# A new hand-written order of the attention turn: where the row maxima, q and k products, statistics and stores stand in each engine's program

## The chip, the cores and the metric

One NeuronCore of one Trainium2 chip runs the whole program. The metric is the device time of one execution in microseconds (us). Five engines run their own instruction streams side by side: TensorE (PE, with its weight loads as PEld), VectorE (DVE), ScalarE (ACT), GpSimd (POOL), and SyncE (SP), which only issues DMAs. They meet through semaphores.

## The reference

A batch of 32 sequences of 512 tokens, 256 channels, float32:

```python
x = x + _layernorm(attn(_layernorm(x)))   # 16 heads of 16, 4 kv groups, rope, causal softmax
x = x + _layernorm(ffn(_layernorm(x)))    # x + shared expert + 2 of 16 experts by sigmoid gates
# attn:  q = rope(x Wq + bq), k = rope(x Wk + bk), v = x Wv + bv; k, v repeated over 4 heads
#        out = softmax(mask(q k^T / 4)) v Wo + bo
# ffn:   gates = sigmoid(x gate_w + gate_b); top 2, weights normalised to sum 1
```

## The kernel before

**Two phases.** `attention_phase` handles attention, the residual, the second layer norm, the router and the scatter of every token to its two experts' lists in DRAM. `expert_phases` then runs the expert tiles and the shared expert. The change touches the first phase alone.

**Turns.** The first phase is one software pipeline over the 32 sequences. Each engine's program is written out by the same loop: for each turn c from -3 to 33, go through the list `TURN`. One turn has 44 slots, (g, e), with g one of 4 kv groups and e one of 11 exponential units. In a full turn the softmax of sequence c stands beside the row maxima of c+1 (groups 1 to 3 of `M` in later slots; group 3 of the own sequence in g = 0), the q, k, v of c+2, the output projection and router of c-1, the scatter of c-2 and the first layer norm of c+3. Every engine is strictly in order, so a slot fixes what stands ahead of what on each engine. The steps of the list:

- `E` (g, e): PE makes scores transposed with the negated maximum already added (L728, L730), three PSUM buffers `ps_a`; ACT takes the exponential (L846).
- `M` (g, u), u = 0 to 5: PE makes the scores of 4 heads (or 2) (L712, L714) into one of two PSUM buffers `ps_d`; DVE reduces them to the row maximum (L966). `MAX_AT` gives each unit's slot.
- `P` (g, j): PE multiplies the exponentials with v (L742); ACT copies the heads out after the last (L889).
- `MISC` places the rest: `xt` (transposes of the normed input), `qe` 0 and 1 (the two halves of q, L758; DVE adds the bias and multiplies with the rope tables, L978), `kk` (k and v, L758; DVE L986, L989), `mt` 0 and 1 (maxima transposed, ACT L856, SP sends them into the operand `qs`), `ot`, `at`, `op` (attention output, L765, L793, L772; DVE L998, L1000, L1004), `ht`, `rg`, `rt` (router), `cn` (places in the lists, L777; DVE L1072 to L1095), `vt`.
- `SIDE` gives the slot of work without PE: DVE's statistics (L939, L947), `add_residual` (two sums of 128x512, L954), `choose`, `weigh_choice`; POOL's `split` (q and k cut into three bf16 parts: L589, L591 or L593, then L585, L587, L585, L587), `root` (L623 to L640), the scatters (L657) and `split_max` (L607 to L613); ACT's `norm` steps (L895); SP's loads and stores.

**Buffers that tie the engines.** `ps_d` has two buffers, so PE may start the n-th step for DVE only when DVE has finished the one two before it:

```python
                if number >= 2:
                    pe.wait_ge(d_taken, number - 1)
```

A scatter of 128 tokens is two indirect DMAs, issued by POOL; there are four scatters (`scatter0` to `scatter3`) in a turn. POOL's `split0a` waits until DVE has taken `qe` 1.

Of the kernel before, what the change touches and what calls it, by code (L numbers as in the profile page):

```python
# [62 lines left out]


MISC = {
    (0, 3): [("xt", 0, 2)],
    (0, 6): [("xt", 1, 2), ("ot", 0, -1), ("ot", 1, -1)],
    (0, 9): [("qe", 0, 2), ("cn", 0, -2), ("at", 0, -1), ("at", 1, -1)],
    (0, 10): [("op", 0, -1)],
    (1, 2): [("op", 1, -1)],  # L70
    (1, 4): [("qe", 1, 2)],
    (1, 7): [("mt", 1, 0)],
    (3, 0): [("kk", 0, 2), ("ht", 0, -1)],
    (3, 2): [("mt", 0, 1), ("ht", 1, -1)],
    (3, 4): [("rg", 0, -1)],
    (3, 7): [("rt", 0, -1)],
    (3, 10): [("vt", 0, 2)],
}

MAX_AT = [[1, 2, 2, 4, 8, 10], [0, 1, 4, 7, 8, 9], [2, 2, 5, 6, 9, 9], [0, 2, 3, 6, 7, 9]]  # L80
SUMS_AT = [10, 4]

SIDE = {
    "load_stacks": (0, 4),
    "load_x_res": (0, 6),
    "load_x": (0, 6),
    "store_q0": (2, 5),
    "store_h2": (3, 8),
    "store_q1": (3, 9),
    "store_k": (3, 10),  # L90
    "scatter0": (0, 9),
    "scatter1": (0, 9),
    "scatter2": (1, 1),
    "scatter3": (1, 3),
    "root_proj": (1, 1),
    "root_2": (2, 3),
    "root_1": (3, 9),
    "split0a": (1, 4),
    "split0b": (1, 7),
    "split0c": (2, 2),  # L100
    "split1a": (2, 4),
    "split1b": (2, 7),
    "split1c": (3, 5),
    "split2a": (3, 7),
# [12 lines left out]
    "plan_limits": (1, 4),
    "stats_proj_a": (1, 3),
    "stats_proj_b": (1, 3),
    "moments_proj": (1, 3),  # L120
    "add_residual_a": (1, 9),
# [4 lines left out]
    "stats_1_a": (2, 10),
    "stats_1_b": (2, 10),
    "moments_1": (3, 1),
    "choose": (3, 8),
# [36 lines left out]
def exists(b):  # L166
    return 0 <= b < B
# [13 lines left out]
A_NO = count_of(FOR_ACT)  # L181
# [132 lines left out]
def attention_phase(nc, a, v):  # L314
# [14 lines left out]
    with ctx:  # L329
# [6 lines left out]
        def sem(name):  # L336
            return ctx.enter_context(nc.semaphore(name))
# [67 lines left out]
        a_full, a_taken = sem("a_full"), sem("a_taken")  # L405
# [521 lines left out]
        def _(dve):  # L927
# [41 lines left out]
            def take(step, arg, b):  # L969
# [11 lines left out]
                elif step == "kk":  # L981
                    if b >= 1:
                        dve.wait_ge(split_steps, SPLITS * (3 * b - 1) + 1)
                    even, odd, both = slice(0, G * DH // 2), slice(G * DH // 2, G * DH), slice(0, G * DH)
                    for dst, src, k in ((roped_k[:, 0, :], both, 2), (roped_k[even, 1, :], odd, 3)):
                        dve.scalar_tensor_tensor(out=dst, in0=ps[src, :], scalar=bk[src, :], in1=rope[src, k, :],  # L986
                                                 op0=ALU.add, op1=ALU.mult)
                    dve.wait_ge(v_t_ready, b + 1)
                    dve.scalar_tensor_tensor(out=roped_k[odd, 1, :], in0=ps[even, :], scalar=bk[even, :],  # L989
                                             in1=rope[even, 3, :], op0=ALU.add, op1=ALU.mult).then_inc(d_taken, 1)  # L990
                elif step == "ot":
                    if arg == 0:
# [741 lines left out]
```

## Time and profile before

| | |
|---|---|
| median of 3 runs | 2605.22 us (2598.71 to 2606.5) |
| profiled execution | 2598.71 us, its span from first to last instruction 2596.9 us |
| share of the span busy | PE 92%, DVE 78%, POOL 63%, ACT 58% |
| granted TensorE clock, mean | 0.965 of full speed (2.4 GHz) |
| turns of the first phase | full turns from about 171 us to 1700 us, 53.4 or 54.9 us each, four of 56.5 to 58.5 us |
| second phase | from about 1850 us |

How to read it: PE's matmuls overlap one another in the records, so that a busy share near 1 does not say how fast it goes; the distance from one matmul's start to the next does. Idle time of an engine stands in square brackets in a timeline, with what ended it.

### The profile page before, as it was taken

How to read it: one execution, taken by the hardware profiler on the slowest of the kernel's cores; microseconds unless marked ns; L12 is line 12 of the kernel's file. 1: busy time of each engine (PE TensorE's matmuls, PEld its weight loads, DVE VectorE, ACT ScalarE, POOL GpSimd, SP SyncE). 2: the span in 40 equal slices, each digit the busy share in tenths (PEclk: the TensorE clock that was granted, in tenths of full speed). 3: DMA queues.
4: the chain of work that ended last, by engine and by line, in shares of the span. 5: the costliest groups of instructions: out<-in, count | busy, mean ns of one | idle time of the engine just before them, and what ended most of it. 6: DMA issues, size and time to landing. Idle time of an engine off the chain costs nothing. (4 is left out here: it accounts for less than half of the span.)

```text
span 2596.9 us, 60759 instructions
## 1 busy us (share of the span) xinstructions
PE 2386.5 (92%) x18798; PEld 1584.4 (61%) x18798; DVE 2025.7 (78%) x5220; ACT 1510.0 (58%) x3420; POOL 1646.0 (63%) x2761
## 2 busy tenths in 40 slices
PE   4999999999999999989999999996389999999997
PEld 2565566655666555555656665563268777877664
DVE  5688888888888888778888888873357777776887
ACT  1566666666766666665666766674134444444664
POOL 2457765666756666666676656734267666766887
PEclk7999999999999999999999999998689999999999
DMA  4354445444445444444443454331346546554997
GB/s 126 107 146 130 130 146 148 149 131 129 146 144 152 132 129 131 137 148 148 124 128 119 139 158 128 115 116 58 78 149 184 155 146 201 160 152 149 315 351 241
DMA packets 288652, 388.00 MB, mean 149 GB/s; under 512 B 27922, under 2 KB 238098, under 8 KB 288212
## 3 DMA queue, kind: packets, MB, share of 16 engines
q1 hardware_dynamic: 260788, 308.56, 40.3%
q0 software_dynamic: 27552, 75.57, 8.5%
q8 instruction: 161, 2.64, 0.4%
q14 instruction: 151, 1.24, 0.2%
HBM read 193.40 MB, written 172.27 MB: 141 GB/s over the span
## 5 line engine op out<-in xcount | busy, mean ns | idle before, releaser
L846 ACT ACTIVATE probs<-ps_a 128x512 f32<-128x512 f32 (+1 forms) x1408 | 718.8, 556 | 415.4 <-PE ps_a L730 398.3
L966 DVE TENSOR_REDUCE negmax<-ps_d 128x2 f32<-128x768 f32 (+3 forms) x768 | 776.9, 1038 | 130.7 <-PE ps_d L714 113.1
L712 PE MATMUL ps_d<-ks,qs 96*128 96x128 bf16 (+3 forms) x2048 | 487.8, 306 | 72.8 <-DVE negmax L966 49.0
L728 PE MATMUL ps_a<-qs,ks 99*128 99x512 bf16 (+3 forms) x2048 | 518.9, 306 | 8.2 <-ACT probs L846 4.4
L730 PE MATMUL ps_a<-mask_exp,ident_bf 128*128 128x128 bf16 x2048 | 398.7, 222 | 0.0
L714 PE MATMUL ps_d<-mask_max,ident_bf 128*128 128x128 bf16 x2048 | 395.5, 222 | 0.0
L1368 POOL DMA_INDIRECT y_dram<-ysb,to_row x286 | 282.4, 987 | 120.3 <-issue 86.3
L198 POOL TENSOR_TENSOR pool_cell<-zero_col 1x1 f32<-1x1 f32 x318 | 58.8, 185 | 463.5 <-DVE slot L1095 405.6
L712 PEld LDWEIGHTS ps_d<-ks,qs 96*128 96x128 bf16 x2048 | 203.4, 99 | 234.8 <-DVE negmax L966 76.2
L742 PE MATMUL ps_out<-probs,va 128*32 128x512 f32 (+3 forms) x4096 | 329.2, 439 | 0.0
L1441 PE MATMUL ps_gu<-wgu,rows_t 128*128 x1144 | 304.0, 389 | 7.1 <-DVE rows_t L1594 3.9
L728 PEld LDWEIGHTS ps_a<-qs,ks 99*128 99x128 bf16 x2048 | 203.1, 99 | 168.0 <-issue 53.9
L657 POOL DMA_INDIRECT sorted_dram<-h,slot x256 | 255.2, 997 | 69.4 <-issue 60.5
L1532 ACT ACTIVATE gate<-ps_gu 128x128 f32<-128x128 f32 x286 | 79.6, 278 | 271.1 <-issue 146.0
L1441 PEld LDWEIGHTS ps_gu<-wgu,rows_t 128*128 128x128 f32 x1144 | 200.6, 196 | 26.0 <-issue 9.4
L730 PEld LDWEIGHTS ps_a<-mask_exp,ident_bf 128*128 128x128 bf16 x2048 | 204.1, 100 | 20.1 <-issue 10.6
L714 PEld LDWEIGHTS ps_d<-mask_max,ident_bf 128*128 128x128 bf16 x2048 | 203.8, 99 | 1.1 <-issue 1.1
L1455 PE MATMUL ps_y<-wd,hid_t 128*128 x572 | 182.0, 400 | 20.9 <-ACT hid_t L1538 17.5
L742 PEld LDWEIGHTS ps_out<-probs,va 128*32 128x32 f32 x4096 | 107.1, 109 | 140.1 <-issue 97.0
L1601 DVE TENSOR_TENSOR hid<-ps_gu,gate 128x128 f32<-128x128 f32 x286 | 83.4, 291 | 123.0 <-ACT gate L1532 106.7
L1594 DVE COPY rows_t<-ps_t 128x256 f32<-128x256 f32 x286 | 118.9, 416 | 35.5 <-PE ps_t L1429 29.4
L585 POOL TENSOR_TENSOR q_parts<-rest,zero_col 128x512 bf16<-128x512 f32 x124 | 138.8, 1119 | 7.3
(200 smaller groups left out, 4585.9 us busy)
## 6 DMA issues: line engine op xcount, KB each, us to landing
qs<-q_stack_dram SPq DMA_DIRECT2D x128, 384.0 KB, 6.1
rows<-sorted_dram SPq DMA_DIRECT2D x286, 129.0 KB
y_in<-y_dram SPq DMA_DIRECT2D x32, 1024.0 KB
q_stack_dram<-q_parts SPq DMA_DIRECT2D x64, 384.0 KB
x_in<-in_x SPq DMA_DIRECT2D x32, 512.0 KB
q_stack_dram<-q_parts SPq DMA_DIRECT2D x64, 256.0 KB
x<-in_x SPq DMA_DIRECT2D x32, 512.0 KB
h_dram<-h SPq DMA_DIRECT2D x32, 512.0 KB, 3.0
```

The source lines that it names most:

```text
L585: steps.did(pool.tensor_tensor(parts[k], r, zero_col[0:n, :].to_broadcast([n, T]), ALU.add))
L657: pool.indirect_dma_start(out=sorted_dram[b // (B // 2)][:, :], in_=h2[:, k, j, :], in_offset=None, out_offset=bass.IndirectOffsetOnAxis(a ...
L712: pe.matmul(ps_d[:, number % 2, at:at + width], qs[0:KR, b % 2, h, j * P:(j + 1) * P], ks[0:KR, b % 2, g, 0:width], start=True, stop=False)
L714: ins = pe.matmul(ps_d[:, number % 2, at + j * P:at + (j + 1) * P], ident_bf[:, :], mask_max[:, :], start=False, stop=True)
L728: pe.matmul(ps_a[:, number % 3, at:at + width], ks[0:KM, b % 2, g, j * P:(j + 1) * P], qs[0:KM, b % 2, g * HG + h0 + k, j * P:T], start=Tr ...
L730: ins = pe.matmul(ps_a[:, number % 3, at:at + P], ident_bf[:, :], mask_exp[:, :], start=False, stop=True)
L742: ins = pe.matmul(ps_out[32 * h:32 * h + 32, j * P:T], va[:, b % 3, j, g * 32:(g + 1) * 32], probs[:, at:at + width], start=(j == 0), stop ...
L846: act.activation(probs[:, at:at + nh * width], ps_a[:, number % 3, 0:nh * width], ACT.Exp) \
L966: dve.tensor_reduce(negmax[:, g // 2, j, at:at + nh], src, AX_X, ALU.max, negate=True) \
L1368: pool.indirect_dma_start(out=y_dram[:, :], in_=ysb[:, k, :], in_offset=None, out_offset=bass.IndirectOffsetOnAxis(ap=to_row[k][:, 0:1].bi ...
L1441: ins = pe.matmul(ps_gu[:, t % 2, 0:2 * I], rows_t[:, t % 2, c, :], wgu[:, expert[t], c, :], start=(c == 0), stop=(c == NC - 1))
L1455: pe.matmul(ps_y[:, t % 2, 0:D], hid_t[:, t % 2, :], wd[:, expert[t], :], start=True, stop=True) \
```

## The change

It moves steps between slots; no operation is added or taken away, and no size changes. One wait of DVE ahead of `ot` is dropped.

```diff
 MISC = {
-    (0, 3): [("xt", 0, 2)],
-    (0, 6): [("xt", 1, 2), ("ot", 0, -1), ("ot", 1, -1)],
-    (0, 9): [("qe", 0, 2), ("cn", 0, -2), ("at", 0, -1), ("at", 1, -1)],
+    (0, 2): [("xt", 0, 2)],
+    (0, 5): [("xt", 1, 2)],
+    (0, 6): [("ot", 0, -1)],
+    (0, 7): [("ot", 1, -1)],
+    (0, 9): [("cn", 0, -2), ("at", 0, -1), ("at", 1, -1)],
     (0, 10): [("op", 0, -1)],
-    (1, 2): [("op", 1, -1)],
-    (1, 4): [("qe", 1, 2)],
-    (1, 7): [("mt", 1, 0)],
-    (3, 0): [("kk", 0, 2), ("ht", 0, -1)],
-    (3, 2): [("mt", 0, 1), ("ht", 1, -1)],
+    (1, 1): [("op", 1, -1)],
+    (1, 7): [("qe", 0, 2), ("qe", 1, 2), ("mt", 1, 0)],
+    (2, 9): [("kk", 0, 2)],
+    (3, 2): [("ht", 0, -1), ("ht", 1, -1)],
     (3, 4): [("rg", 0, -1)],
-    (3, 7): [("rt", 0, -1)],
-    (3, 10): [("vt", 0, 2)],
+    (3, 7): [("mt", 0, 1), ("vt", 0, 2)],
+    (3, 8): [("rt", 0, -1)],
 }
-MAX_AT = [[1, 2, 2, 4, 8, 10], [0, 1, 4, 7, 8, 9], [2, 2, 5, 6, 9, 9], [0, 2, 3, 6, 7, 9]]
+MAX_AT = [[0, 0, 1, 3, 8, 10], [0, 1, 3, 6, 8, 9], [0, 1, 4, 6, 7, 9], [1, 1, 3, 7, 8, 8]]
 SIDE = {
-    "load_stacks": (0, 4),        "load_x": (0, 6),
+    "load_stacks": (0, 5),        "load_x": (0, 5),
-    "store_q0": (2, 5),   "store_h2": (3, 8),   "store_q1": (3, 9),   "scatter1": (0, 9),
+    "store_q0": (2, 4),   "store_h2": (3, 10),  "store_q1": (3, 10),  "scatter1": (0, 10),
-    "root_proj": (1, 1),  "root_2": (2, 3),     "root_1": (3, 9),
+    "root_proj": (1, 2),  "root_2": (2, 6),     "root_1": (3, 10),
-    "split0a": (1, 4),    "split0b": (1, 7),
+    "split0a": (1, 2),    "split0b": (1, 9),
-    "split1a": (2, 4),    "split1b": (2, 7),    "split1c": (3, 5),    "split2a": (3, 7),
+    "split1a": (2, 7),    "split1b": (3, 2),    "split1c": (3, 7),    "split2a": (3, 9),
-    "norm_proj_a": (1, 7),     "norm_proj_b": (1, 7),
+    "norm_proj_a": (1, 9),     "norm_proj_b": (1, 9),
-    "weigh_choice_a": (0, 0),  "weigh_choice_b": (0, 1),   "plan_limits": (1, 4),
+    "weigh_choice_a": (0, 2),  "weigh_choice_b": (0, 5),   "plan_limits": (1, 3),
-    "stats_proj_a": (1, 3),    "stats_proj_b": (1, 3),     "moments_proj": (1, 3),
+    "stats_proj_a": (1, 2),    "stats_proj_b": (1, 4),     "moments_proj": (1, 5),
-    "add_residual_a": (1, 9),  "stats_2_b": (1, 10),
+    "add_residual_a": (1, 10), "stats_2_b": (2, 0),
-    "stats_1_a": (2, 10),      "stats_1_b": (2, 10),       "moments_1": (3, 1),  "choose": (3, 8),
+    "stats_1_a": (3, 4),       "stats_1_b": (3, 4),        "moments_1": (3, 6),  "choose": (3, 10),
 }
@@ DVE, step "ot" @@
                         post.begin(b)
-                        if exists(b + 3):
-                            dve.wait_ge(a_taken, A_NO["xt", 1, b + 3] + 1)
```

Unchanged entries are left out and several stand on one line. `scatter0` (0, 9), `scatter2` (1, 1), `scatter3` (1, 3), `split0c` (2, 2), `add_residual_b` and `stats_2_a` (1, 10), `moments_2` (2, 4), `norm_2` (2, 10), `norm_1_a` (3, 8), `norm_1_b` and `split2b`, `split2c` (3, 10) stay.

## Rows read from the trace of the kernel before

**Rows 1.** The page: span and busy time by engine.

```profile
span 2596.9 us, 60759 instructions
PE 2386.5 (92%) x18798; PEld 1584.4 (61%) x18798; DVE 2025.7 (78%) x5220; ACT 1510.0 (58%) x3420; POOL 1646.0 (63%) x2761
```

**Rows 2.** Windows, one whole turn each: us, busy by engine, PEclk, DMA.

```profile
1324.30:1377.70 53.40, 51.71 (x485) 32.48 (x483) 46.13 (x101) 36.14 (x73) 35.45 (x59) 1.00 0.46 135
1377.70:1432.60 54.90, 53.24 (x485) 33.39 (x483) 46.07 (x101) 36.19 (x73) 36.48 (x60) 0.97 0.44 132
```

**Rows 3.** PE's timeline in the turn from 1324.30.

```profile
1349.69 0.38 PE L712 MATMUL ps_d<-ks,qs 96*128 96x512 bf16 x1
...
1353.53 0.38 PE L728 MATMUL ps_a<-qs,ks 99*128 99x512 bf16 x1
1353.92 0.39 PE L728 MATMUL ps_a<-qs,ks 99*128 99x512 bf16 x1
1354.40 0.39 PE L728 MATMUL ps_a<-qs,ks 99*128 99x512 bf16 x1
...
1357.21 0.34 PE L728 MATMUL ps_a<-qs,ks 99*128 99x384 bf16 x1
...
1358.84 0.34 PE L712 MATMUL ps_d<-ks,qs 96*128 96x384 bf16 x1 [1.24 <-DVE negmax L966]
...
1359.97 0.34 PE L712 MATMUL ps_d<-ks,qs 96*128 96x384 bf16 x1 [0.29 <-DVE negmax L966]
...
1365.50 1.93 PE L758 MATMUL ps_d<-h1t,wkv 128*128 128x512 f32 x4
1367.27 0.60 PE L797 MATMUL ps_a<-ident,h 128*128 128x128 f32 x4
```

**Rows 4.** DVE's timeline in the same turn.

```profile
1330.97 0.36 DVE L998 RECIPROCAL denom<-ps_d 128x32 f32<-128x32 f32 x1 [0.81 <-PE ps_d L765]
1331.37 0.69 DVE L1000 TENSOR_TENSOR h_heads<-ps_d,denom 128x512 f32<-128x512 f32 x1
...
1348.25 1.28 DVE L978 SCALAR_TENSOR_TENSOR roped_q<-ps_d,bq,rope 128x1024 f32<-128x1024 f32 x1
1349.45 3.35 DVE L966 TENSOR_REDUCE negmax<-ps_d 128x2 f32<-128x768 f32 x3
1352.94 3.82 DVE L954 TENSOR_TENSOR x<-proj,x 128x512 f32<-128x512 f32 x2
1356.79 1.41 DVE L939 BATCH_NORM_STATS2 stats<-x 128x6 f32<-128x256 f32 x4
1358.12 1.80 DVE L966 TENSOR_REDUCE negmax<-ps_d 128x4 f32<-128x512 f32 x2
```

**Rows 5.** POOL's timeline in the same turn.

```profile
1351.08 1.09 POOL L657 DMA_INDIRECT sorted_dram<-h,slot  x1 [0.29 <-POOL shift L640]
1352.48 0.97 POOL L657 DMA_INDIRECT sorted_dram<-h,slot  x1 [0.30 <-issue]
1353.47 1.28 POOL L589 TENSOR_TENSOR rest<-roped_q 128x512 f32<-128x512 f32 x1
1354.83 1.38 POOL L585 TENSOR_TENSOR q_parts<-rest,zero_col 128x512 bf16<-128x512 f32 x1
...
1357.86 1.04 POOL L585 TENSOR_TENSOR q_parts<-rest,zero_col 128x512 bf16<-128x512 f32 x1
```

**Rows 6.** The line of the residual (L954): all, and after 1720 us.

```profile
L954 DVE TENSOR_TENSOR x<-proj,x x64: 682/1524/2374, 147.4 to 1811.9; 128x512 f32<-128x512 f32 x64
...
L954 DVE TENSOR_TENSOR x<-proj,x x6: 682/688/693, 1725.5 to 1811.9; 128x512 f32<-128x512 f32 x6
```

**Rows 7.** DVE's and POOL's timelines near 1725 us, where no split follows the scatter.

```profile
1725.49 1.29 DVE L954 TENSOR_TENSOR x<-proj,x 128x512 f32<-128x512 f32 x2 [0.29 <-ACT proj L895]
...
1725.03 0.97 POOL L657 DMA_INDIRECT sorted_dram<-h,slot  x1 [0.30 <-issue]
```

**Rows 8.** ACT's timeline: the norm of the projection.

```profile
1350.83 2.08 ACT L895 ACTIVATE proj<-proj,shift,rstd 128x256 f32<-128x256 f32 x4 [0.69 <-POOL shift L640]
```

More of the change, by code:

```diff
@@ L65 @@
 MISC = {
-    (0, 3): [("xt", 0, 2)],
-    (0, 6): [("xt", 1, 2), ("ot", 0, -1), ("ot", 1, -1)],
-    (0, 9): [("qe", 0, 2), ("cn", 0, -2), ("at", 0, -1), ("at", 1, -1)],
-    (0, 10): [("op", 0, -1)],
-    (1, 2): [("op", 1, -1)],
-    (1, 4): [("qe", 1, 2)],
-    (1, 7): [("mt", 1, 0)],
-    (3, 0): [("kk", 0, 2), ("ht", 0, -1)],
-    (3, 2): [("mt", 0, 1), ("ht", 1, -1)],
+    (0, 2): [("xt", 0, 2)],
[3 more added lines that the diff above has]
+    (0, 9): [("cn", 0, -2), ("at", 0, -1), ("at", 1, -1)],
+    (0, 10): [("op", 0, -1)],
+    (1, 1): [("op", 1, -1)],
+    (1, 7): [("qe", 0, 2), ("qe", 1, 2), ("mt", 1, 0)],
+    (2, 9): [("kk", 0, 2)],
+    (3, 2): [("ht", 0, -1), ("ht", 1, -1)],
     (3, 4): [("rg", 0, -1)],
-    (3, 7): [("rt", 0, -1)],
-    (3, 10): [("vt", 0, 2)],
+    (3, 7): [("mt", 0, 1), ("vt", 0, 2)],
+    (3, 8): [("rt", 0, -1)],
 }
-MAX_AT = [[1, 2, 2, 4, 8, 10], [0, 1, 4, 7, 8, 9], [2, 2, 5, 6, 9, 9], [0, 2, 3, 6, 7, 9]]
+MAX_AT = [[0, 0, 1, 3, 8, 10], [0, 1, 3, 6, 8, 9], [0, 1, 4, 6, 7, 9], [1, 1, 3, 7, 8, 8]]
 SUMS_AT = [10, 4]
 SIDE = {
-    "load_stacks": (0, 4),
+    "load_stacks": (0, 5),
     "load_x_res": (0, 6),
[L86 to L89, printed above, removed]
+    "load_x": (0, 5),
+    "store_q0": (2, 4),
+    "store_h2": (3, 10),
+    "store_q1": (3, 10),
     "store_k": (3, 10),
     "scatter0": (0, 9),
-    "scatter1": (0, 9),
+    "scatter1": (0, 10),
     "scatter2": (1, 1),
     "scatter3": (1, 3),
[L95 to L99, printed above, removed]
+    "root_proj": (1, 2),
+    "root_2": (2, 6),
+    "root_1": (3, 10),
+    "split0a": (1, 2),
+    "split0b": (1, 9),
     "split0c": (2, 2),
[L101 to L104, printed above, removed]
+    "split1a": (2, 7),
+    "split1b": (3, 2),
+    "split1c": (3, 7),
+    "split2a": (3, 9),
     "split2b": (3, 10),
     "split2c": (3, 10),
-    "norm_proj_a": (1, 7),
-    "norm_proj_b": (1, 7),
+    "norm_proj_a": (1, 9),
+    "norm_proj_b": (1, 9),
     "norm_2_a": (2, 10),
@@ L112 @@
     "norm_1_b": (3, 10),
-    "weigh_choice_a": (0, 0),
-    "weigh_choice_b": (0, 1),
+    "weigh_choice_a": (0, 2),
+    "weigh_choice_b": (0, 5),
     "plan_ends": (0, 9),
     "plan_tiles": (1, 0),
[L117 to L121, printed above, removed]
+    "plan_limits": (1, 3),
+    "stats_proj_a": (1, 2),
+    "stats_proj_b": (1, 4),
+    "moments_proj": (1, 5),
+    "add_residual_a": (1, 10),
     "add_residual_b": (1, 10),
     "stats_2_a": (1, 10),
-    "stats_2_b": (1, 10),
+    "stats_2_b": (2, 0),
     "moments_2": (2, 4),
[L126 to L129, printed above, removed]
+    "stats_1_a": (3, 4),
+    "stats_1_b": (3, 4),
+    "moments_1": (3, 6),
+    "choose": (3, 10),
 }
```

## The prediction

> **What bounds the kernel now.** The page first [rows 1]: PE is busy for 2386.5 us of the 2596.9 and DVE for 2025.7. A busy share says little of PE, so I cut the first phase into its turns with the windows view [rows 2]. Most full turns take either 53.4 or 54.9 us; the longer ones show a granted clock of 0.97 instead of 1.00, which is a stretch at 1.2 GHz for 1.5 us more. DVE is busy for 46.1 us of either. There are 28 full turns (c = 2 to 29) of sequences alike.
>
> Then PE's timeline in one 53.4 us turn [rows 3]. I give times as offsets from the turn's start, 1324.30. PE runs without a hole up to the maxima of slot (1, 8), at 25.4. Behind them it falters: three exponential units start 0.39, 0.48 and 0.29 apart, where 0.28 is the unhindered distance, and then it waits for DVE's maxima, so that steps 0.22 apart start 1.63 and 0.67 apart. That is 0.1 + 0.2 + 1.4 + 0.45, with 0.2 ahead of the first unit and 0.1 later: 2.4 us lost in this stretch and some 0.3 us in the rest of the turn. PE alone would need 50.7 us.
>
> Why DVE is late stands in its timeline [rows 4]: at offset 28.6 it begins the residual, two sums, which take 3.82 us; then statistics, and the maxima for which PE waits only come behind them. The line's own view shows that this is not what the sums need [rows 6]: a median of 1524 and up to 2374 ns over all, 682 to 693 after 1720 us. POOL's timeline has the reason [rows 5]: while DVE sums, POOL works on tensors in SBUF. The first sum starts at 28.64 and can't end before POOL's subtraction (29.17 to 30.45) is over; the second waits for POOL's next. Near 1725 us no split follows the scatter, and two sums take 1.29 us together although an indirect DMA runs beside them [rows 7]. So the two engines exclude one another on such instructions, and indirect DMAs don't count. The turn is PE's 50.7 us plus what this collision makes PE wait.
>
> **The change part by part.** The number of instructions and their sizes don't change, so PE's 50.7 us stay. The question is only how far PE slips behind its own pace.
>
> *Start of the turn.* Maxima go one slot earlier and `weigh_choice` later. PE's `ot` 0 ends at 6.6 at its new offset, DVE is through with its four maxima and the weights by then (they fill 6.0 us of the timeline now), and takes 0.36 + 0.69 us for it [rows 4], so it is done by 7.8; PE wants its buffer for the next maxima at 7.9. At most 0.1 us is lost here. `qe` 0 leaves this part, and `op` follows the counts directly; between them PE's positions only move by the 1.77 us of one q product (the k product has that distance [rows 3]). The dropped wait costs and gains nothing: PE's `ot` stands behind `xt` 1 anyway.
>
> *The two q products side by side.* The steps ahead of slot (1, 8) are the same set as before, so PE reaches it at the same offset, 25.3. Back from there, `qe` 1 starts at 22.85, lasts 1.97, and DVE takes it from 24.9 to 26.15 (1.28 [rows 4]). Two maxima follow (three take 3.35 us [rows 4], the narrow one 0.95 of it) and end at 28.5. The earlier of the two buffers is free in time for each; nothing is lost.
>
> *ACT's norm of the projection* moves behind one more pair of exponentials, to slot (1, 9). Its last exponential ends near 26.9, and the norm takes 2.08 us [rows 8], so that DVE's residual can start at 29.0, 0.4 later than now. In exchange PE's 0.3 us of faltering at the exponentials goes, since these are now taken in time.
>
> *POOL.* It is in order, and `split0a` now stands ahead of `scatter3`, waiting for `qe` 1 until 26.15. So: 1.28 us of split to 27.5, 0.29 of idle, the first indirect DMA 1.09, 0.30 of idle, the second from about 29.2 to 30.2 [rows 5], and at once `split0b` (1.04). The scatters ahead of it and `root_proj` end near 24.5, in time.
>
> *The residual, then, against POOL.* This decides. The first sum (29.0) starts 0.2 us before the second indirect DMA. Before the change it started 0.46 us after that DMA's start and still lost to the tensor instruction that stood behind the DMA, though that one only starts 0.53 us later in the records [rows 4, 5]. POOL must have had its claim in as soon as the DMA was under way. By that, the first sum now wins and ends at 29.6, the second finds the claim of `split0b` and waits until 31.2, and with its last 0.56 us ends at 31.8. The Trainium skill ("SBUF — State Buffer", "SBUF: two separate sides") calls the shared port pair an exclusive lock that whichever instruction starts first holds for the whole of it. The exclusion agrees with rows 4 to 6; "starts first" does not agree with the recorded starts there, 0.53 us the other way.
>
> *From there to the k product.* DVE: two statistics (0.7) to 32.5, M(1,0) done 33.2, two statistics 33.8, M(1,1) done 35.0, M(1,2) 35.8, moments (0.3), M(1,3) 37.0, M(1,4) 38.2 [rows 4]. PE may start M(1,2) when M(1,0) is done: it wants to at 32.2 and slips 1.0; M(1,3) behind M(1,1): slip 1.95; M(1,4) behind M(1,2): 2.15. New is that `kk` stands at (2, 9), inside the stretch where DVE is behind, and waits for M(1,4): slip 2.7. After it PE works 1.77 us on a product and DVE catches up; statistics of x, now at (3, 4), fall into DVE's idle time there. What stood in their old place saves DVE 1.35 us, but only after `kk`.
>
> *The rest.* `mt` 0 goes from (3, 2) to (3, 7); it is copied, sent and needed 4.8 us later at the next turn's start, where `mt` 1 now has 4.5 and costs PE 0.2 at most. POOL's `root_1` goes behind `split2a` and ends 0 to 0.3 us before ACT wants it for `norm_1_a`. If POOL were 1 us later there, ACT would stand still for that time, with three `ps_a` buffers of cover. The stores and loads of the stacks shift by under 1 us, with over 2 us of room before group 0's maxima. In sum the turn loses 2.7 us instead of 2.4 + 0.3: 53.4 us, as before. Holes of 2.7 us as close together as now let the clock fall about as often.
>
> **The rivals.** (A) The forecast above, no change: 2598.7 us of the profiled execution, give or take 15 us, which is 0.5 us a turn for steps that I placed by 0.2 or 0.3 us each. (B) Both sums win. The second starts at 29.6, before the recorded start of `split0b` at 30.2. If POOL's claim is not made before 0.4 us into its last DMA, or by any rule that goes by recorded starts, the residual ends at 30.2, PE slips only 1.1 us in the turn (M(1,3) 0.3, M(1,4) 0.5, `kk` 1.1). That is 1.6 us less in 28 turns, 45 us, and the lower clock of some third of the turns would largely go, another 10: 2545 us. By the skill's rule, named above, it would be this case. For it: the claim is only bounded, somewhere in the first 0.5 us. Against: the one geometry that the trace has went POOL's way in all full turns. (C) Both sums lose: if the norm ends 0.3 us later, or POOL's scatter 0.3 us earlier than I placed them, the first sum meets a claimed port, waits for `split0b` to 31.2, ends at 31.8, and the second waits for a further subtraction and ends at 33.4. PE slips 4.3 us by `kk`: 1.6 us more in 28 turns, 45 us, 2645 us. It decides from a shift of 0.2 to 0.3 us between ACT and POOL, which is the uncertainty of both chains. This is the case on the slow side. (D) The edits don't act at all: excluded where DVE is the limit.
>
> **How the numbers follow.** A 0.45, B 0.22, C 0.28, others (ACT standing before `root_1`, a stack late, the four long turns with the pad rows coming out otherwise, 15 us among them) 0.05. A measurement tells 0.3%, 8 us, from no change. A is centred on no change with a spread of 15 us: 0.17 faster, 0.15 same, 0.13 slower. With B and C: faster 0.41, same 0.17, slower 0.42. The runs' median is 2605.2 us, 6.5 above the profiled execution, and a new median should lie between: 2602 us. The range holds A and most of B and C: 2540 to 2655; A alone would be 2587 to 2618.
>
> **What would show it.** In the trace after: the residual line's durations. About 690 ns for the first sum and 2200 for the second is A; 690 for both is B; both over 2000 is C. PE's waits for DVE at L712 between offsets 32 and 38, four smaller ones instead of two, and one at L758 ahead of the k product. POOL's `split0a` directly behind DVE's second q step. The turn's length by windows: 53.4, 51.8 or 55.0. I am wrong in kind if PE waits elsewhere: for ACT at the end of a turn, or for `ot`'s buffer near offset 8.

## The result, and the profile of the kernel after

The change makes the kernel slower by 0.9%: 2626.75 us (median of 4 runs, 2620.0 to 2629.71) against 2605.86 of the kernel before beside it, ratio 1.0091 with a 95% interval of 1.0068 to 1.0113. Run once more in another job (e13 below) it gave 1.0060 (1.0040 to 1.0080). The forecast was no change, 2602 us.

The page and the windows of two full turns stand first. The page: span and busy time.

```profile
span 2619.1 us, 60730 instructions
PE 2389.8 (91%) x18798; PEld 1576.4 (60%) x18798; DVE 1981.9 (76%) x5220; ACT 1510.6 (58%) x3420; POOL 1637.4 (63%) x2761
```

Windows of the kernel after, columns as in [rows 2]: two full turns, and the turns 17 to 21 together.

```profile
1341.70:1395.80 54.10, 52.12 (x488) 32.40 (x485) 44.48 (x103) 36.21 (x74) 35.20 (x59) 1.00 0.45 134
1395.80:1449.80 54.00, 51.98 (x487) 32.31 (x483) 44.34 (x101) 36.09 (x74) 35.08 (x59) 1.00 0.45 133
...
sum 294.50, PE 268.10 PEld 167.66 DVE 226.43 ACT 181.18 POOL 191.59; mean PE 53.62 PEld 33.53 DVE 45.29 ACT 36.24 POOL 38.32
```

The same five turns of the kernel before, as one sum of windows:

```profile
sum 285.80, PE 264.65 PEld 165.71 DVE 233.84 ACT 181.17 POOL 191.84; mean PE 52.93 PEld 33.14 DVE 46.77 ACT 36.23 POOL 38.37
```

DVE is busy for 44 us less in all and PE ends 22.2 us later. A full turn at full clock takes 54.04 us (from its first E matmul to the next turn's) instead of 53.41 [rows 2]. But in turns 2 to 16 the kernel before had 8 stretches at the lower clock (54.9 us turns), the kernel after 4. So those fifteen turns take 813.7 us before and 815.1 after. The 22.2 us lie here: turns -2 to 1 +6.7, turns 2 to 16 +1.4, turns 17 to 21 +8.7, turns 22 to 29 +3.6, the rest +1.8. These are net figures. At full clock a full turn is 0.63 us longer, which is 14.5 us over the 23 plain ones (turns 2 to 16 and 22 to 29); the lower clock, met less often, gave back 9.5 of them. Of the 8.7 us of turns 17 to 21, 3.2 are the same 0.63 us again and 4.3 fell in turn 18 alone (58.6 us before, 62.9 after). So the longer full turn is the largest part, 17.6 us over all 28, and the start the next.

One full turn after, from 1341.70. First PE: the maxima M(0,3) and the heads' product P(0,3), both q products, and the waits further on.

```profile
1361.04 0.86 PE L743 MATMUL ps_out<-probs,va 128*32 128x256 f32 x16
...
1362.67 0.22 PE L715 MATMUL ps_d<-mask_max,ident_bf 128*128 128x128 bf16 x1
...
1365.17 1.98 PE L759 MATMUL ps_d<-h1t,wq 128*128 128x512 f32 x4 [0.28 <-DVE negmax L967]
...
1367.76 0.38 PE L713 MATMUL ps_d<-ks,qs 96*128 96x512 bf16 x1
...
1375.48 0.34 PE L713 MATMUL ps_d<-ks,qs 96*128 96x384 bf16 x1 [0.64 <-DVE negmax L967]
1377.27 0.34 PE L713 MATMUL ps_d<-ks,qs 96*128 96x384 bf16 x1 [0.72 <-DVE negmax L967]
1380.40 1.98 PE L759 MATMUL ps_d<-h1t,wkv 128*128 128x512 f32 x4 [0.31 <-DVE negmax L967]
```

DVE's timeline in the same turn:

```profile
1364.16 0.96 DVE L967 TENSOR_REDUCE negmax<-ps_d 128x2 f32<-128x768 f32 x1 [0.82 <-PE ps_d L715]
...
1367.19 1.28 DVE L979 SCALAR_TENSOR_TENSOR roped_q<-ps_d,bq,rope 128x1024 f32<-128x1024 f32 x1 [0.89 <-PE ps_d L759]
...
1371.44 2.61 DVE L955 TENSOR_TENSOR x<-proj,x 128x512 f32<-128x512 f32 x2 [0.57 <-ACT proj L896]
```

POOL's, with `scatter1` and `scatter2` now four indirect DMAs in a row:

```profile
1358.23 0.99 POOL L658 DMA_INDIRECT sorted_dram<-h,slot  x1 [0.15 <-issue]
1359.53 0.96 POOL L658 DMA_INDIRECT sorted_dram<-h,slot  x1 [0.31 <-issue]
1360.79 0.96 POOL L658 DMA_INDIRECT sorted_dram<-h,slot  x1 [0.30 <-issue]
1362.06 0.96 POOL L658 DMA_INDIRECT sorted_dram<-h,slot  x1 [0.30 <-issue]
...
1371.45 0.97 POOL L658 DMA_INDIRECT sorted_dram<-h,slot  x1 [0.30 <-issue]
1372.43 1.06 POOL L586 TENSOR_TENSOR q_parts<-rest,zero_col 128x512 bf16<-128x512 f32 x1
```

and ACT's copy of the heads behind P(0,3):

```profile
1364.01 0.59 ACT L890 COPY heads_t<-ps_out 128x512 f32<-128x512 f32 x1 [2.35 <-remote]
```

The collision came as forecast in case A: of the two sums in the 2.61 us, the first took 728 ns and the second 1955, and PE waits at M(1,2), M(1,3) and the k product. What was not forecast stands ahead of it. M(0,3) ends at 1362.89 by the records and DVE, idle since 1363.33, takes it at 1364.16, 1.27 us after that end. P(0,3) ends at 1361.90 and ACT, idle, copies at 1364.01, 2.11 us after. For most steps of the turn an idle engine starts 0.04 to 0.07 us behind PE's end. Both late starts come after POOL's row of four indirect DMAs has ended (1363.02). Through them the second q product waits 0.28 us, M(0,4) starts at offset 26.06 instead of 25.39 [rows 3], and the residual at 29.74 instead of the forecast 29.0.

A row of four is not new: the kernel before has one too (`scatter0` and `scatter1`), further ahead in its turn. POOL's last DMA of it, PE's second `op`, and DVE's start behind that:

```profile
1343.07 0.96 POOL L657 DMA_INDIRECT sorted_dram<-h,slot  x1 [0.30 <-issue]
```

```profile
1342.41 1.94 PE L772 MATMUL ps_d<-wo,headst_h2t 128*128 128x256 f32 x8
```

```profile
1344.85 0.69 DVE L1004 TENSOR_TENSOR proj<-ps_d,bo 128x512 f32<-128x512 f32 x1 [1.02 <-PE ps_d L772]
```

DVE starts 0.50 us after PE's recorded end there, and ACT's copy behind P(0,3) comes 0.4 us late in most full turns. So late starts were there before the change; the change moved the row to where they are longer and where M(0,3) and P(0,3) stand.

The start, in windows (turns -1 and 0), of before and then of after:

```profile
24.50:72.60 48.10, 25.72 (x126) 13.03 (x126) 32.50 (x48) 2.78 (x6) 16.07 (x24) 0.71 0.42 127
72.60:119.00 46.40, 44.25 (x401) 25.82 (x400) 31.56 (x39) 29.59 (x59) 23.71 (x34) 0.97 0.38 107
```

```profile
23.40:73.70 50.30, 25.98 (x127) 13.21 (x126) 33.06 (x48) 2.98 (x6) 15.52 (x21) 0.66 0.38 112
73.70:124.10 50.40, 47.40 (x401) 27.42 (x402) 31.89 (x39) 28.76 (x57) 22.71 (x35) 0.90 0.36 104
```

In turn -1 PE has little to do and stands for the first stacks, 15.3 us before. The first q product stood ahead of that wait and now stands behind it, and turn 0 runs at a granted clock of 0.90 instead of 0.97.

### The profile page after: what moved, and what is told of

Same layout as the page of the kernel before. It is cut to its first block and busy times, and to the rows that moved or that the text cites. A ratio compares the mean times of both kernels' runs of the same rounds, so it can differ in the third digit from the quotient of the medians.

```text
span 2619.1 us, 60730 instructions
## 1 busy us (share of the span) xinstructions
PE 2389.8 (91%) x18798; PEld 1576.4 (60%) x18798; DVE 1981.9 (76%) x5220; ACT 1510.6 (58%) x3420; POOL 1637.4 (63%) x2761
## 5 line engine op out<-in xcount | busy, mean ns | idle before, releaser
L847 ACT ACTIVATE probs<-ps_a 128x512 f32<-128x512 f32 (+1 forms) x1408 | 736.8, 561 | 354.1 <-PE ps_a L731 288.0
L729 PE MATMUL ps_a<-qs,ks 99*128 99x512 bf16 (+3 forms) x2048 | 525.4, 304 | 1.4 <-ACT probs L847 0.3
L1440 PEld LDWEIGHTS ps_gu<-wgu,rows_t 128*128 128x128 f32 x1144 | 200.1, 195 | 30.6 <-issue 14.5
L1621 DVE SCALAR_TENSOR_TENSOR ysb<-ps_y,rows,half_row 128x256 f32<-128x256 f32 x286 | 138.4, 484 | 9.7 <-PE ps_y L1454 3.6
```

Source lines behind the costliest of these rows:

```text
L729: pe.matmul(ps_a[:, number % 3, at:at + width], ks[0:KM, b % 2, g, j * P:(j + 1) * P], qs[0:KM, b % 2, g * HG + h0 + k, j * P:T], start=Tr ...
L847: act.activation(probs[:, at:at + nh * width], ps_a[:, number % 3, 0:nh * width], ACT.Exp) \
L1440: ins = pe.matmul(ps_gu[:, t % 2, 0:2 * I], rows_t[:, t % 2, c, :], wgu[:, expert[t], c, :], start=(c == 0), stop=(c == NC - 1))
L1621: dve.scalar_tensor_tensor(out=ysb[:, k, :], in0=ps_y[:, t % 2, 0:D], scalar=rows[:, t % RD, D + 1:D + 2], in1=half_row[:, t % 2, :], op0= ...
```

## The experiments

Ratios are to the kernel before, run beside each kernel in its job. "The wait" is one line in `split`, ahead of POOL's next step against the residual; `x1_ready` counts finished sums.

**e1: POOL waits for the residual, in the kernel after.**

```diff
+                if stage == 1 and unit == 0 and 0 <= b - 3 < B:
+                    pool.wait_ge(x1_ready, 2 * (b - 2))
```

> The kernel after, and POOL waits for both sums of the residual before it begins the split of the k heads' first part (split0b). Port theory (the turn after loses its time because the second sum stands behind a subtraction of POOL, 728 and 1955 ns in the turn from 1341.7): both sums take about 690 ns, the residual 1.4 us in all, the maxima behind it come 1.3 us sooner, PE's waits for DVE in slots (1, 8) to (2, 9) mostly go (0.64 + 0.72 + 0.31 + what the steps between them lose), so a full turn goes from 54.0 to 52.4 us, and over 28 turns some 45 us come off: about 2580 us. Rival (late signals: the turn after lost its 0.6 us because PE's signals reach DVE 1 to 2 us late behind four indirect DMAs in a row, and the residual only fills time that PE lacks anyway): the sums shorten, but DVE's later start of the maxima stays; 53.5 us or more a turn, under 15 us off in all.

2585.76 us, 0.9918 (0.9899 to 0.9936). Both sums take 732 and 679 ns, and a full turn 52.67 us instead of 54.04. The port theory holds: the blocked sum costs 1.37 us a turn. Some of the gain is lost in turn 18, which takes 71.5 us here and 62.9 in the kernel after; it holds a DMA wait that differs from run to run (see e14 and the section on the forecast).

**e2: the same in the kernel before**, with `stage == 0`, ahead of `split0a`.

> The kernel before, and POOL waits for both sums of the residual before it begins split0a, which stands next to the residual there. Port theory: the two sums of 3.82 us become 1.4, PE's 1.24 and 0.29 us of waiting for the maxima go with what the steps between lose (2.4 us in the turn), and a turn is 53.4 - 2.0 = 51.4 us, 28 turns 55 us less: about 2545 us. If the collision costs PE nothing net (POOL's chain, later by up to 1.3 us, becomes what is waited for: root_2, split0c or split1), the turn stays at 53 us or more, 2590 us or more.

2584.96 us, 0.9907 (0.9889 to 0.9926). The sums take 693 and 684 ns, and M(1,5) comes 1.77 us sooner, but a full turn takes 53.31 us: only 0.1 less than a turn at full clock before. What the whole gains is that no turn up to 16 is of the 54.9 us kind now. ACT's timeline, PE's and POOL's show where the 1.77 us went:

```profile
1359.69 1.58 ACT L897 ACTIVATE h<-x,shift,rstd 128x256 f32<-128x256 f32 x3 [1.98 <-POOL shift L642]
```

```profile
1361.90 0.63 PE L799 MATMUL ps_a<-ident,h 128*128 128x128 f32 x4 [0.57 <-ACT h L897]
1364.61 0.38 PE L817 MATMUL ps_a<-ident_bf,negmax_parts 128*24 128x128 bf16 x4 [0.85 <-POOL negmax_parts L615]
```

```profile
1350.28 1.27 POOL L591 TENSOR_TENSOR rest<-roped_q 128x512 f32<-128x512 f32 x1 [0.96 <-DVE x L956]
```

POOL begins its row of splits and roots at offset 30.3 instead of 29.15, and works without a hole of note to the root that the norm of x needs. ACT waits for POOL, and PE for both.

**e8: e2, and `ht` 0 and `mt` 0 to later slots.**

```diff
-    (3, 0): [("kk", 0, 2), ("ht", 0, -1)],
-    (3, 2): [("mt", 0, 1), ("ht", 1, -1)],
+    (3, 0): [("kk", 0, 2)],
+    (3, 2): [("ht", 0, -1), ("ht", 1, -1)],
-    (3, 7): [("rt", 0, -1)],
+    (3, 7): [("mt", 0, 1), ("rt", 0, -1)],
```

> The kernel before with POOL's wait (e2), and ht 0 moved from (3, 0) to (3, 2) and mt 0 from (3, 2) to (3, 7), as in the change. In e2 the shorter residual brought PE 1.77 us by slot (2, 9), and PE gave 0.57 us of it back waiting for ACT at ht 0 and 0.85 us waiting for POOL's split of the maxima at mt 0. If those two places are where the gain went, the full turns go from 53.3 to about 51.9, 28 turns 39 us less: about 2545 us. If POOL's later chain binds at other places too (split1, the norm of the next sequence), 52.5 or more.

2585.65 us, 0.9935 (0.9905 to 0.9965), full turns of 53.34. The expectation fell. PE's 0.85 us at `mt` 0 are gone, but at `ht` it now waits 0.52 us for ACT's exponentials and early in the turn 0.48 us for DVE, and ACT waits 0.96 us instead of 0.37 for POOL at the norm of the next sequence. The two places only showed the limit; that POOL's chain of about 53.3 us sets it is what e15 tests.

**e15: the kernel before, third scatter behind the root** (`"scatter2": (1, 2)`).

> The kernel before with the third scatter behind the root of the projection. POOL's root ends near 26.0, two scatters follow to 31.3, and split0a begins at 31.4 instead of 29.2; both sums (28.6 and 29.2) come before POOL's last indirect DMA and take 690 ns each. Theory drawn from e2 and e8 (there POOL worked without a hole from the residual to the norm of x and set a turn of 53.3): its row of work now begins 1.1 us later than in e2, so the turn is 53.3 to 54.4 and the kernel no faster than before, 2590 to 2630 us. Rival (the port alone is what cost the kernel before its 2.4 us a turn, as the forecast had it): turns of 51.7, about 2555 us.

2632.85 us, 1.0078 (1.0060 to 1.0096). Full turns take 54.4 or 55.0, with both sums undisturbed (DVE) and ACT waiting 3.11 us for POOL, whose split begins at 31.4 or 32.0:

```profile
1377.22 1.28 DVE L954 TENSOR_TENSOR x<-proj,x 128x512 f32<-128x512 f32 x2
```

```profile
1390.05 2.08 ACT L895 ACTIVATE h<-x,shift,rstd 128x256 f32<-128x256 f32 x4 [3.11 <-POOL shift L640]
```

The turn's length follows POOL one for one: the split begins 1.13 or 1.73 us later than in e2, and the turns are 1.13 or 1.72 us longer. The whole came out just above the expected 2590 to 2630 us. With e2 and e8 this shows that in the old order POOL's chain is a second bound right under the collision. Freeing DVE alone gives nearly nothing.

**e3: the first q product back in (0, 9), in the kernel after.**

```diff
-    (0, 9): [("cn", 0, -2), ("at", 0, -1), ("at", 1, -1)],
+    (0, 9): [("qe", 0, 2), ("cn", 0, -2), ("at", 0, -1), ("at", 1, -1)],
-    (1, 7): [("qe", 0, 2), ("qe", 1, 2), ("mt", 1, 0)],
+    (1, 7): [("qe", 1, 2), ("mt", 1, 0)],
```

> The kernel after with one part undone: the first q product stands in slot (0, 9) again. If the start-up pays for its move (turn -1 took 50.25 us after and 48.09 before, PE stood for 17.92 us at one place instead of 15.29), 2 us come back at the start. If M(0, 3)'s late signal (1.27 us in the full turns) delays the second of two q products side by side, the full turns gain the 0.3 to 0.5 us by which DVE's second q step came late: 54.0 to 53.6 us, 10 us in all. Together about -12 us, 2615 us. If the pair of q products was not at fault, only the 2 us of the start.

2603.35 us, 0.9992 (0.9975 to 1.0009): this one move is worth the whole 0.9%. It also gave a comparison that no one had to build: full turns of two lengths side by side, at full clock. Windows:

```profile
1372.40:1424.80 52.40, 52.06 (x488) 32.33 (x484) 43.05 (x102) 36.13 (x74) 35.03 (x59) 1.00 0.47 138
1424.80:1478.80 54.00, 51.99 (x488) 32.42 (x485) 44.22 (x103) 36.01 (x74) 35.05 (x59) 1.00 0.45 134
```

DVE's residual in each, then POOL beside it:

```profile
1401.79 1.29 DVE L955 TENSOR_TENSOR x<-proj,x 128x512 f32<-128x512 f32 x2 [0.44 <-issue]
...
1454.66 2.41 DVE L955 TENSOR_TENSOR x<-proj,x 128x512 f32<-128x512 f32 x2 [0.57 <-ACT proj L896]
```

```profile
1402.05 1.27 POOL L658 DMA_INDIRECT sorted_dram<-h,slot  x1 [0.30 <-issue]
1403.33 1.06 POOL L586 TENSOR_TENSOR q_parts<-rest,zero_col 128x512 bf16<-128x512 f32 x1
...
1454.48 0.96 POOL L658 DMA_INDIRECT sorted_dram<-h,slot  x1 [0.30 <-issue]
1455.47 1.05 POOL L586 TENSOR_TENSOR q_parts<-rest,zero_col 128x512 bf16<-128x512 f32 x1
```

In the short turn the second sum starts 0.34 us after POOL's last indirect DMA and takes 684 ns; in the long one it starts 0.8 us after and takes 1806. The turns differ by 1.6 us, the forecast's distance from case A to B. With the residual's 0.5 us goes the heads' copy behind P(0,3), which comes 1.0 to 1.8 us after PE's end in the short turns and 2.4 or 2.5 in the long ones. What decides between the two is not shown.

**e5: e1 and e3 together.**

> The kernel after with both of the edits that gained alone: POOL waits for the residual before split0b (e1), and the first q product stands in (0, 9) again (e3). e3 had full turns of two kinds, 52.4 us where both sums took 690 ns and 54.0 where the second took 1810. If the port alone makes the difference between them, all full turns are now 52.4 or, as e1's 0.2 us wait at the second q product goes too, 52.2; over e1 (52.66) that is 8 to 13 us and 2 us at the start: about 2573 us. If the two edits gain the same time twice (the q products' DVE step late only moved the residual), it stays at e1's 2586.

2570.91 us, 0.9871 (0.9827 to 0.9914). The total is what was expected, but not for the reasons given: full turns take 52.85, longer than e1's, since `mt` 1 waits 0.51 us for ACT behind the late heads' copy. The gain over e1 is the start (157.6 us for turns -2 to 1 instead of 164.1) and turn 18 (61.4 instead of 71.5).

**e4: the k product back in (3, 0), in the kernel after.**

> The kernel after with one part undone: the k product stands in slot (3, 0) again, behind the maxima of group 2. If its place inside the stretch where DVE is behind costs PE what its wait shows (0.31 us in the turn from 1341.7, and by the forecast 0.55 us more slip than at M(1, 4)), the full turns gain 0.3 to 0.5 us, 8 to 14 us in all, about 2615 us. If the slip is only handed on to the next maxima, no change within 0.2%.

2657.64 us, 1.0208 (1.0181 to 1.0235), the other way: full turns of 55.2. The maxima of group 2 had been pulled forward with the k product. With the product right ahead of them, PE waits for DVE to take k before it may start M(2,1):

```profile
1410.61 0.28 PE L713 MATMUL ps_d<-ks,qs 96*128 96x256 bf16 x1 [1.61 <-DVE roped_k_v_t L990]
```

**e6 and e9: the third scatter behind POOL's root of the projection**, e6 with e1's wait and e9 without.

```diff
-    "scatter2": (1, 1),
-    "root_proj": (1, 2),
+    "scatter2": (1, 2),
+    "root_proj": (1, 1),
```

> As e1, and the third scatter goes behind POOL's root of the projection, so that no more than two indirect DMAs stand in a row beside PE's signals of P(0, 3) and M(0, 3), where e1 has four. Theory of late signals (a row of indirect DMAs keeps PE's signals from the engines that wait): the heads' copy behind P(0, 3) and the maxima behind M(0, 3), which start 2.03 and 1.18 us after the matmul's end in e1, start under 0.5 us behind it; the maxima come 0.7 us sooner, PE's 0.2 us wait at the second q product goes, and the turn is 52.3 to 52.5 instead of 52.66. Rival (the delay belongs to the place in the turn, not to the row): both stay above 1 us. A cost that may hide the gain: split0a and the last scatter come 0.4 us later.

> The kernel after with one move: the third scatter stands behind POOL's root of the projection, as in e6, but without the wait of POOL for the residual. It tells whether the row of four indirect DMAs is the first cause, and the lost second sum its consequence. In e6 the sums began at 29.2 and 29.8 and POOL's last indirect DMA at 30.2, so that both were ahead of it, and POOL's wait cost nothing. If that holds without the wait, full turns take 52.2 us instead of 54.0, and the whole is about 2565 us. If the wait was what saved the sums, one of them takes over 1500 ns again and a turn is 53.5 or more, about 2605 us.

e6: 2566.35 us, 0.9836 (0.9791 to 0.9881). e9: 2567.32 us, 0.9841 (0.9821 to 0.9860). Both have full turns of 52.17 us, all alike. In e9's turn from 1306.0, PE, then DVE, ACT and POOL:

```profile
1325.28 0.86 PE L743 MATMUL ps_out<-probs,va 128*32 128x256 f32 x16
...
1326.91 0.22 PE L715 MATMUL ps_d<-mask_max,ident_bf 128*128 128x128 bf16 x1
```

```profile
1335.13 1.29 DVE L955 TENSOR_TENSOR x<-proj,x 128x512 f32<-128x512 f32 x2 [0.57 <-ACT proj L896]
```

```profile
1326.20 0.59 ACT L890 COPY heads_t<-ps_out 128x512 f32<-128x512 f32 x1 [0.30 <-PE ps_out L743]
```

```profile
1323.76 0.96 POOL L658 DMA_INDIRECT sorted_dram<-h,slot  x1 [0.30 <-issue]
1327.66 0.20 POOL L624 TENSOR_TENSOR var<-moments,eps 128x4 f32<-128x4 f32 x1 [2.94 <-DVE moments L948]
...
1336.12 1.14 POOL L658 DMA_INDIRECT sorted_dram<-h,slot  x1 [0.30 <-issue]
1337.28 1.05 POOL L586 TENSOR_TENSOR q_parts<-rest,zero_col 128x512 bf16<-128x512 f32 x1
```

The copy now follows P(0,3)'s end (1326.14) by 0.06 us instead of 2.11, and DVE's start behind M(0,3) is not late either. The residual begins at offset 29.2, a microsecond ahead of POOL's last indirect DMA, both sums run free, and the wait is not needed. What the late starts cost by themselves is the distance from e1 to e6, where both sums are free in either: 0.50 us a turn. The other 1.37 us of the 1.87 is the blocked sum. Breaking up the row frees it too, but e9 moves two things toward that: the first sum comes 0.5 us sooner (the late starts gone), and POOL's last indirect DMA 0.4 us later (30.14 instead of 29.75, since the third scatter now stands behind the root). That the blocked sum was a consequence of the late starts alone is therefore not shown.

**e10: e9 with e3's move and the pads of e7 (below).**

> As e9, with the pad rows apart (e7) and the first q product in (0, 9) again (e3, e5). The pads took 11 us off the turns 19 to 21 in e7 and the place of the q product 5 to 7 us off the start in e3 and e5; in e5 the full turns lost 0.5 us by ACT's heads copy coming 2.4 us behind P(0, 3), a late signal that e9's move should take away. If the three are independent: e9 less 16 to 18 us, about 2548, and full turns of 52.2 or less. If the q product in (0, 9) makes the full turns longer by itself, they are over 52.4 and the whole is above 2553.

2607.28 us, 1.0001 (0.9989 to 1.0012), full turns of 53.81, the slow rival. With the q product ahead of `cn`, the places in the lists come later, and POOL's work behind them too, the first scatter by 2.7 us and the last by 2.3. Its `split0a` now meets the first sum, as in the kernel before (DVE, then POOL):

```profile
1363.56 2.37 DVE L956 TENSOR_TENSOR x<-proj,x 128x512 f32<-128x512 f32 x2 [0.57 <-ACT proj L897]
```

```profile
1363.50 1.28 POOL L591 TENSOR_TENSOR rest<-roped_q 128x512 f32<-128x512 f32 x1
```

**e7: the pad rows apart, in the kernel after.** Turns 18 to 21 each hold four more indirect DMAs, which fill the lists' ends.

```diff
+PAD_AT = ((0, 2), (1, 2), (2, 5), (3, 10))
-                    if B // 2 + 2 <= c < B // 2 + 6 and at in ((0, 2), (0, 4), (0, 6), (0, 8)):
-                        pad(4 * (c - B // 2 - 2) + at[1] // 2 - 1)
+                    if B // 2 + 2 <= c < B // 2 + 6 and at in PAD_AT:
+                        pad(4 * (c - B // 2 - 2) + PAD_AT.index(at))
```

> The kernel after, and the four indirect DMAs of pad rows in each of the turns 18 to 21 no longer stand in a row at the start of the turn but singly: in (0, 2), behind the root of the projection in (1, 2), in (2, 5) and in (3, 10), where POOL has idle time. These turns and turn 17 took 294.5 us after and 285.8 before, against 270 for five plain ones. If rows of indirect DMAs are what delays PE's signals (7.3 and 6.1 us in turn 18, 2.9 in turns 19 to 21), the five turns take 275 to 280 and the whole 15 to 20 us less, about 2610 us. If the long turns come from something else (the experts' weights, the store that the first pad waits for), they stay above 290.

2606.12 us, 0.9998 (0.9979 to 1.0017). Turns 19 to 21 take 54.4 to 54.7 us instead of 58.1 to 58.5, turn 18 stays at 62.7. There PE waits for something else:

```profile
1066.92 0.27 PE L714 MATMUL ps_d<-ks,qs 96*128 96x128 bf16 x1 [6.15 <-DMA qs<-q_stack_dram]
```

**e11: e10, and the pad row's two stores one turn earlier** (`if c == E:` for `if c == E + 1:`).

> As e10, and SP issues the two stores of the pad row one turn earlier. Turn 18 took 58.6 us before, 62.9 after and 62.7 with the pads apart (e7), and its first pad began at 10.7 us behind the store. If the wait for the store makes turn 18 long (the pads can't run in POOL's idle time at the turn's start, so that they stand in a row with the scatters), it takes 53 to 55 us as its neighbours do in e7, and the whole 7 to 9 us less than e10. If turn 18 is long for the experts' weights or the plan, nothing changes.

2606.00 us, 0.9992 (0.9981 to 1.0004). Turn 18 takes 64.6 us, e10's 66.3: it was not that store.

**e14: e9, the pads apart, and the first plan's store by SP moved from the start of turn 18, ahead of the stacks' loads, to slot (1, 4).**

> e9 (the third scatter behind the root) with the pads apart (e7), and SP stores the first half's plan in slot (1, 4) of turn 18 instead of at its start, ahead of the stacks' loads. Full turns 52.2 as in e9. Turns 19 to 21 took 57.1, 58.1 and 58.1 in e9; apart, 53 each, as e7's were 0.5 over its plain turns: 14 us less. If the plan's store is what held up the stacks in turn 18 (6.2 us of PE's waiting in e7), that turn goes from 62.3 to 54 to 56. Together 2543 to 2547 us. If turn 18 stays at 60 or more, it was not the plan's store, and the sum is 2552.

2561.14 us, 0.9803 (0.9784 to 0.9823). Windows of turns 18 and 19:

```profile
1017.60:1072.30 54.70, 52.11 (x488) 32.35 (x485) 43.41 (x102) 35.20 (x72) 37.82 (x60) 1.00 0.55 144
1072.30:1128.60 56.30, 52.56 (x488) 32.35 (x485) 44.39 (x102) 35.88 (x73) 39.08 (x63) 1.00 0.46 138
```

Turn 18 falls from 62.3 (e9) to 54.7. In e7, with the pads apart alone, it had not moved, and in e17 and e18 below, which also move the store, it takes 56.4 and 57.1, where every run without that edit has 58.6 or more. So the plan's store was its cause. Turns 19 to 21 stay at 56.3, where 53 were expected: in this order POOL has no hole late in the turn, and PE waits 0.8 to 0.9 us for ACT at three places behind the pads.

**e17, e18: e14 with two pads at the start of each of eight turns**, slots (0, 2) and (0, 4) of turns 18 to 25; the same kernel in two jobs.

> e14 with the sixteen pad rows otherwise: two in each of the turns 18 to 25, both at the turn's start in slots (0, 2) and (0, 4), where POOL has over 9 us of idle time in e9, instead of four singly in four turns. In e14 the turns 19 to 21 still took 56.3 against 52.2, with PE waiting 0.8 to 0.9 us for ACT at three places, as the pad in (3, 10) stands ahead of the root that ACT's norm waits for, and those in (1, 2) and (2, 5) push POOL's splits. If that is their cost, two pads in idle time cost under 0.5 us a turn: turns 18 to 25 take 53.5 for turn 18 and 52.2 to 52.7 for the others, and the whole is 2545 to 2550. If a row of two already delays PE's signals by 2 us, as four do, they take 54 or more and it is 2557 or above.

> e17's kernel once more. In e17's job the kernel before took 2560 us instead of 2606 and the second phase 738 us instead of 764 to 772, so that the length of its turns can't be held against e14's. If the kernel before comes out near 2606 here and the turns 19 to 25 still take 52.2 to 52.7, two pads in idle time cost nothing, and the whole is 2545 to 2550, a ratio of 0.976 to 0.979. If the turns 19 to 25 take 53.5 or more here, it was the job that made them short, and a row of two already has a price.

2511.56 us, 0.9803 (0.9782 to 0.9825), and 2515.75 us, 0.9812 (0.9799 to 0.9825). The kernel before took 2560 and 2563 us in these two jobs, so the ratios alone can be held against the others. Turns 19 to 25 take 52.17 to 52.24 in both, like the plain ones, and turns -2 to 32 end 12 to 15 us sooner than e14's; what follows them took 738 and 741 us, and 763 to 772 in all other jobs. Two pads in idle time cost nothing in these two jobs. That can't be held against e14, for in these two jobs, which ran on other chips than the rest, no start is late. Of 1236 and 1241 waits of ACT and DVE for PE the latest ends 0.15 and 0.13 us after PE's recorded end, in the second phase too. In each of the other traces 83 to 163 such waits end later than 0.15 us, the latest 1.35 to 2.75. ACT in the same place of turn 12, behind the same row of two, first in e14 (0.62 us after PE's end at 731.62) and then in e17 (0.03 us after 730.39):

```profile
732.24 0.60 ACT L852 ACTIVATE probs<-ps_a 128x512 f32<-128x512 f32 x1 [0.73 <-PE ps_a L736]
```

```profile
730.42 1.08 ACT L851 ACTIVATE probs<-ps_a 128x512 f32<-128x512 f32 x2 [0.36 <-PE ps_a L735]
```

The 46 us that the kernel before took less there, and the shorter second phase, would fit, but neither of the two kernels compared was profiled in such a job, and the kernel after was not run in one. So whether the change costs 0.9% where no start is late is open, and so is why the ratio is no better than e14's.

**e12, e16, e13: the dropped wait of DVE back, twice, and the kernel after once more.**

> The kernel after with the dropped wait of DVE ahead of ot put back, all else as after. By the forecast it costs and gains nothing, since PE's ot stands behind xt 1 in either order: ratio to after 1.000, 2625 us give or take 5. If DVE's wait for ACT delays ot's start (the maxima of group 3 stand behind it), a turn gets 0.1 us longer or more, 2629 or above.

> The kernel after, unchanged, beside the others of this job. If the first measurement holds: ratio to before 1.007 to 1.011. If the job matters more than its interval says, it comes out near e12's 1.004.

> The kernel after with DVE's dropped wait put back, once more, beside e13. If the wait costs and gains nothing, its ratio to before is within 0.2% of e13's; if it saves 0.5% as e12 suggested, it is 0.4 to 0.6% below e13.

With the wait: 2617.59 us, 1.0038 (1.0025 to 1.0052), and 2623.67 us, 1.0048 (1.0032 to 1.0063). Without it, beside the latter: 2628.17 us, 1.0060 (1.0040 to 1.0080). The intervals overlap, full turns are 53.96, 54.04 and 54.04 us: no difference can be told. The first measurement of the kernel after (1.0068 to 1.0113) lies above both of those with the wait, but its own repeat came out 0.3% lower, so the job matters as much.

## Why the forecast was wrong, step by step

**"Two q products side by side, nothing is lost": the step that failed.** It holds the full turn at 53.4 us; measured are 54.04, and 0.63 us in 28 turns are 17.6 of the 22.2 us. PE reached M(0,4) 0.67 us late, because DVE and ACT started 1.3 and 2.1 us late behind POOL's row of four indirect DMAs. The forecast had no term for that, though the kernel before shows starts 0.3 to 0.5 us late around its own row. With the row broken up (e9) the same two products side by side cost nothing, and with them apart but the row kept (e3) 14 of the 23 plain full turns still take 53.9 to 54.1 us.

**The sum's reach: failed too.** 28 full turns were costed, and the rest was left unchanged, with the long turns only a part of a spread. The start cost 6.7 us. It is not chance: turns -2 to 1 took 164 to 168 us in eleven runs with both q products at (1, 7) (172 in e4), 159 to 162 in the four with the old order, and 158 to 164 in those with `qe` 0 back (e3, e5, e10, e11). It was in reach of the profile before: a windows row for turn -1, and the question what stands ahead of the long wait there. Of the 8.7 us in turns 17 to 21 less can be laid to the change. Turn 18, 4.3 of them, took 62.9 to 66.3 us in four runs of the new order without other edits that touch it (after, e12, e13, e16), and in the four of the old order 58.6, 64.6, 67.2 and 70.8 (before, e8, e15, e2), so its 4.3 us lie within the spread of one DMA wait.

**"The clock falls about as often": failed, and hid part of the rest.** 8 turns in turns 2 to 16 before, 4 after, and one more before in the turns behind 21. This gave back 9.5 us. That the whole came out only 0.9% from "no change" is in that part luck.

**The residual against POOL: right.** "The first sum wins, the second waits": 690 and 2200 ns forecast, 728 and 1955 measured, alike in the other full turns, and PE's waits at the three steps named. Case B, both free, was forecast at 1.6 us a turn less and came so in e3 (1.6), at 52.17 in e9 against a forecast of 51.8. Case C, both lost, came nowhere; in e10 the first sum alone is lost. The forecast took the claim to be made at once or within 0.4 us of POOL's DMA; e3's free sum at 0.34 us and the lost one of before at 0.46 [rows 4, 5] put it between. That A came is in part luck: by the forecast's own times the second sum starts 0.4 us behind POOL's DMA, where neither run decides, and by the trace 0.65 us behind, since the first sum slipped by 0.7 us and the DMA by 0.55.

The Trainium skill ("SBUF — State Buffer", "SBUF: two separate sides") has the pair go to the operation that starts first. In e3's short turn and in e9 that agrees with the records. It does not for the sum that loses in e3's long turn, which starts 0.2 us ahead of the split in the records.

**"The turn is PE's 50.7 us plus what this collision makes PE wait": wrong for the kernel before.** e2 took the collision away there and the turn fell by 0.1 us. A timeline shows which wait ends last, not which chain comes next; POOL's row was not summed. The new order did lower that second bound (e1: 52.67 with the same wait), which the forecast gave no credit.

**`kk` in (2, 9):** the slip was forecast to grow by 0.55 us there; PE waits 0.31. That its old place would be dearer (e4, 1.1 us a turn) was not seen. **The dropped wait** costs nothing that can be measured: right.

## What to carry to other kernels

Before summing a change over the steady turns, make the same sum for the first turns and for each turn that differs; here the start alone was 6.7 of 22.2 us. Compare like with like: net sums over turns at two clocks hid that the longer full turn was the largest part. When a stall is to be removed, sum the row of work behind the engine that waits for it: e1 and e2 are the same line, and it freed 1.4 us a turn in one order and 0.1 in the other. The best version measured breaks up the row of indirect DMAs, puts the pads in idle time and moves one store behind the loads that PE waits for: 0.980 of the kernel before (e14), the new order with e9's move alone 0.984.

## What the runs showed of the hardware

**Rows of indirect DMAs and PE's consumers.** Behind four in a row, an idle ACT and DVE started 2.0 to 2.3 and 1.2 to 1.4 us after PE's recorded ends, in 27 turns each of the kernel after; around the row of the kernel before 0.3 to 0.5 us. In e9, with rows of two, the same copy of ACT came 0.07 us behind PE, but an exponential beside the last row still 0.6. In turns 19 to 21 ACT's copy came 2.9 us behind P(3,3) where four pads stand in a row, and 0.5 us where they stand apart (e7). In e17 and e18, with the same rows of two, no start is late at all, so it depends on the job or chip as well. The runs show that the row's length and place decide in the other jobs. They don't show whether the signal is held up, or the matmul's end: the Trainium skill ("Perfetto Trace Analysis", "Tensor Engine Instruction (MATMUL, LD_WEIGHTS)") says that PE's ends are estimated and that the semaphore goes out only when PSUM has acknowledged the write. It gives no length for that, and no run here separates the two.

**The port from the other side.** POOL's indirect DMA takes 0.96 us, and 1.27 (e3's short turn), 1.14 (e9) and 1.36 (e15) where DVE's sums run beside it. DVE's sums are hardly slowed by the DMA: 684 to 693 ns in most cases, and 720 to 732 where sum and DMA start together (the first sum in the kernel after and e1). The Trainium skill ("SBUF — State Buffer", "A bandwidth-pool intuition that's wrong (but worth ruling out)") has a DMA of GpSimd wait for descriptors while DVE holds the pair; the trace agrees in kind, with 0.2 to 0.4 us.
